# A fused four-block attention kernel: the gates of groups 0 and 1 share one switch of ScalarE's tables inside the FFN, q of group 1 and k's transposes move into the middle of round 0, and the last FFN rows move back

## The chip, the cores and the metric

The kernel runs on one core of a Trainium2 chip. The metric is the device time of one execution in microseconds (us); lower is better. TensorE is PE, VectorE is DVE, ScalarE is ACT, GpSimd is POOL.

## The reference

The input `x` is 32 sequences of 64 tokens with 128 features (2,048 tokens). It passes four blocks:

```python
x = L0(x, ctx)   # layer norm, cross attention, 16 heads of 8, quantised weights
x = L1(x, ctx)   # self attention, cross attention, FFN 128 -> 512 -> 128 with gelu; a layer norm after each
x = L2(x, ctx)   # a gate, three iterations of which only the last counts:
                 #   fused = text + sigmoid(Wg_t @ text_proj + Wg_v @ (r * vision) + bg) * (r * vision)
                 #   with r = softmax over the 64 tokens of 2 * agreement; then a layer norm
x = L3(x, ctx)   # rms norm, rope attention (16 heads of 64, 4 kv heads), rms norm, silu MLP 128 -> 512 -> 128
```

## The kernel before

The tokens are cut into eight groups (`NG`) of 256 tokens (`TG` = 2 tiles of 128). Every engine has a list of steps that is written out by hand and runs in that order; engines meet at semaphores alone, and a step that waits holds all that stands behind it on its engine.

1. L0 and the two attentions of L1 take 24 passes, up to about 220 us of the trace. The change does not touch them.
2. The FFN of L1 follows, group by group. PE runs `mlp_in(g)` (two transposes), `mlp_up(g)` (L531) and `mlp_down(g)` (L544); ACT copies (`f_in`, L858) and takes `gelu(g)` (L867); DVE adds, takes statistics (`ffn_sum`, L1325 and L1275 to L1280) and writes the normed rows (`ffn_rows`, L1334 and L1339) once POOL has the root (L1660). `FT` = 4 tiles of 128 make the 512.
3. Between them PE fills banks with work of the next blocks for the first groups (the tables `EARLY_A`, `EARLY_B`). `RAMP` brings in group 0's q.
4. Then come rounds. Round r has two halves; each does one tile of 128 tokens of L3's attention for group r. It also does L2 for group r + 2, q for group r + 1 and the MLP of group r - 1. `OPENING` lists the two halves of round 0, `HALVES` those of all later rounds, which are alike.

The names in these tables, each with its PE work, its reader and what stands between:

- `l_in`, `l_text`, `l_gate`, `l_back`: L2. PE transposes x (L610), multiplies (L639), multiplies for agreement and gate (L646, L648). ACT copies the bank (`read`, L981, L983, L987). Then `l2_max` (DVE, L1399), `l2_exp` (ACT, L921), `l2_gate` (DVE, L1409), `l2_logits` (POOL, L1813 and L1816), `l2_tanh` (ACT, L930), `l2_weigh` (DVE, L1418), `l2_fuse` (POOL, L1823 and L1827); `l_back` transposes the result `fus` back, and `l2_stats`, `l2_rstd`, `l2_rows` norm it (DVE, POOL, DVE). Group g needs all of these, one after another.
- `k`, `v` (L625), then rope on k: `rotate_k` (DVE, L1477 and L1480), `sum_k` (POOL, L1802 and L1805), and the transposes `kt`, `ks` on PE (L610), copied by ACT (L995).
- `in`: rms norm of L3: `sq3` (ACT, L941), `rms_mean` (DVE, L1449), `rms_power` (POOL), `rms` (ACT, L959), two transposes, a copy (L975). `q0` to `q3` (PE, L617) need it, and DVE reads each with rope (L1463).
- `s0`, `s1`: scores of one tile (PE, L713 to L733) into two banks. `smax3` (DVE, L1519 and L1521), `exps3` (ACT, L1014), `sum3` (DVE), `probs3` (POOL, L1786), `t0`, `t1` (PE transposes, L742), `evac_t3` (ACT, L1020), `pv0`, `pv1` (PE, L756), `evac_pv3` (ACT, L1027), `out` (PE, L633), read by DVE (L1485).

PSUM has eight banks. From `RAMP` on, the uses take them in a ring (`RING3`), so each use waits until the use eight places ahead of it has been read; the early uses take two banks in turn:

```python
def ring_bank(n):
    return (4, 7)[n % 2] if n < NEARLY else RING3[(n - NEARLY) % len(RING3)]
```

Gelu and exp lie in different tables of ACT. The program holds an ACT_TABLE_LOAD where the set changes. Tanh runs after either without a load of its own, as the lists below show.

Of the kernel before, what the change touches and what calls it, by code (L numbers as in the profile page):

```python
# [28 lines left out]
NG = B // GB  # L29
# [57 lines left out]
def build(nc, dr, out):  # L87
    with ExitStack() as ctx:
# [106 lines left out]
        sq = sb("sq", [128, 2, D])  # L195
        ss3 = sb("ss3", [128, 2, TG])
# [36 lines left out]
        def row(name, n=TG):  # L233
# [558 lines left out]
        def _(act):  # L792
# [237 lines left out]
            def opening():  # L1030
                exps3(0)
                l2_tanh(1)
                read("v", 1)
                exps3(1)
                read("k", 2)
                read("l_in", 2)
                read("v", 2)
                exps3(2)
                read("l_back", 1)
                exps3(3)  # L1040
                evac_t3(0)
                read("l_text", 2)
                evac_t3(1)
                read("l_gate", 2)
                sq3(1)
                l2_exp(2)
                evac_pv3(0)
                evac_pv3(1)
                rms(1)
                read("in", 1)  # L1050
                l2_tanh(2)
                evac_t3(2)
# [4 lines left out]
            def first_half(r):  # L1057
# [4 lines left out]
                if 1 <= r < NG - 1:  # L1062
                    sq3(r + 1)
# [68 lines left out]
            l2_exp(0)  # L1132
            f_in(5)
            read("l_in", 1)
            gelu(4)
            l2_tanh(0)
            read("kt", 0)
            f_in(6)
            read("ks", 0)
            gelu(5)  # L1140
            read("l_text", 1)
            read("k", 1)
            gelu(6)
# [17 lines left out]
        def _(dve):  # L1161
# [395 lines left out]

            def first_half(r):
# [400 lines left out]
```

## Time and profile before

| what | us |
|---|---|
| median of 3 runs (502.46 to 503.14) | 502.51 |
| the profiled execution, its own time | 503.35 |
| its span, first to last instruction | 501.4 |
| busy in the span: PE, DVE | 451.1, 377.4 |
| busy in the span: ACT, POOL | 298.6, 273.3 |

1.95 us of the profiled execution's time lie outside its span, and the profiled execution is 0.84 us above the median. "Busy" for PE counts modelled ends of pipelined matmuls, so PE's start times are the better measure: the distance from one start to the next is what a step costs PE. Each fp32 matmul of the program appears twice in the trace (two passes), so a step of four matmuls shows as x8. A row's bracket is the idle time of the engine ahead of it and who ended it.

### The profile page before, as it was taken

Reading aid. Unit: us, or ns where it says so; the run is one execution under the profiler, and the core shown is the slowest. Engines: PE = TensorE matmul, PEld = TensorE weight load, DVE = VectorE, ACT = ScalarE, POOL = GpSimd, SP = SyncE. Lnnn points to the kernel's source line nnn. Section 1 sums busy time; section 2 is a strip of 40 time slices with the busy share of each in tenths; the row PEclk is TensorE's granted clock in tenths of the full one; section 3 lists DMA queues with packets and bytes.
Section 4 is the critical chain, followed back from the end, with each engine's and each line's share of the span. In section 5 each row is a group of like instructions: output and inputs, shape, how many; then the busy total and the mean of one; then the engine's idle time right before and its main releaser. Section 6 shows DMA issues by size and latency. Waiting matters only on the chain.

```text
span 501.4 us, 16946 instructions
## 1 busy us (share of the span) xinstructions
PE 451.1 (90%) x6872; PEld 358.1 (71%) x6872; DVE 377.4 (75%) x918; ACT 298.6 (60%) x724; POOL 273.3 (54%) x332
## 2 busy tenths in 40 slices
PE   4798899999998999899968598999999999999885
PEld 4466666766666776688866377888888888878674
DVE  6699877688988888887687765868777677867642
ACT  2377676767777776757743536565565556553531
POOL 6464877579867787964443534445353545431210
PEclk9799999999999999999989698999999999999999
DMA  8970000000000000000000000000000000000000
GB/s 273 237 244 3 2 3 3 2 3 3 1 4 3 2 3 3 1 1 2 2 0 3 2 1 2 3 12 3 12 3 1 13 3 12 1 13 3 14 1 21
DMA packets 12420, 11.54 MB, mean 23 GB/s; under 512 B 5176, under 2 KB 10296, under 8 KB 12344
## 3 DMA queue, kind: packets, MB, share of 16 engines
q1 hardware_dynamic: 11624, 9.01, 6.9%
q10 hardware_dynamic: 720, 1.45, 0.8%
q8 instruction: 55, 0.90, 0.8%
q14 instruction: 21, 0.17, 0.1%
HBM read 9.42 MB, written 1.05 MB: 21 GB/s over the span
## 4 chain that ended last, share of the span: by engine, by line
PE 49%; DVE 25%; issue 14%; POOL 6%; ACT 4%; DMA 1%; DVEq 0%; POOLq 0%; ACTq 0%
DVE negm L1244 8%; PE ps L617 5%; PE ps L633 5%; DVE blocks L1235 5%; PE ps L733 5%; PE ps L447 4%; PE ps L655 4%; PE ps L465 3%; PE ps L625 2%; PE ps L610 2%; PE ps L495 2%; PE ps L663 2%; PE ps L756 2%; PE ps L407 2%; PE ps L408 2%
## 5 line engine op out<-in xcount | busy, mean ns | idle before, releaser
L1244 DVE TENSOR_REDUCE negm<-ps 128x8 bf16<-128x512 f32 x96 | 59.6, 683 | 25.2 <-PE ps L447 25.1
L832 ACT ACTIVATE p<-ps 128x512 f32<-128x512 f32 x96 | 54.5, 595 | 28.2 <-PE ps L455 27.1
L838 ACT ACTIVATE shared<-ps 128x512 f32<-128x512 f32 x96 | 57.0, 601 | 21.7 <-PE ps L465 20.3
L1733 POOL TENSOR_TENSOR wide<-wide,cv 128x1024 f32<-128x1024 f32 x24 | 45.6, 1901 | 32.6 <-ACT wide L822 32.6
L465 PE MATMUL ps<-cst,p 128*128 128x128 f32 x384 | 58.5, 276 | 0.4 <-ACT shared L838 0.4
L1660 POOL TENSOR_TENSOR rstd<-veps,neghalf 128x2 f32<-128x2 f32 x40 | 29.5, 738 | 49.2 <-DVE veps L1280 30.7
L1786 POOL TENSOR_TENSOR probs<-p,rc 128x512 f32<-128x512 f32 x32 | 33.0, 1044 | 40.6 <-DVE rc L1530 40.5
L465 PEld LDWEIGHTS ps<-cst,p 128*128 128x128 f32 x384 | 44.2, 141 | 11.5 <-issue 9.4
L1027 ACT ACTIVATE late<-ps 128x512 f32<-128x512 f32 x32 | 17.3, 592 | 31.5 <-PE ps L756 31.5
L633 PEld LDWEIGHTS ps<-wo,late 128*128 128x128 f32 x256 | 33.5, 206 | 3.5 <-issue 2.8
L633 PE MATMUL ps<-wo,late 128*128 128x128 f32 x256 | 33.9, 290 | 2.2 <-ACT late L1027 2.2
L617 PE MATMUL ps<-shared,wq 128*128 128x256 f32 x128 | 30.6, 383 | 3.5 <-ACT shared L975 3.4
L1519 DVE TENSOR_REDUCE mx<-ps 128x8 f32<-128x512 f32 x32 | 21.9, 686 | 15.5 <-PE ps L733 15.5
L455 PE MATMUL ps<-negm,idb 128*128 128x512 bf16 x96 | 29.2, 383 | 4.7 <-DVE negm L1244 4.7
L655 PE MATMUL ps<-in_t,wg 128*128 128x256 f32 x128 | 30.0, 380 | 0.7 <-ACT in_t L977 0.7
L617 PEld LDWEIGHTS ps<-shared,wq 128*128 128x128 f32 x128 | 23.1, 190 | 7.5 <-issue 3.3
L1235 DVE TENSOR_TENSOR blocks<-ps,rv 64x128 f32<-64x128 f32 x96 | 27.4, 286 | 1.0
L479 PEld LDWEIGHTS ps<-shared,blocks 128*32 128x32 f32 x1536 | 22.5, 110 | 7.6 <-ACT shared L838 6.4
L447 PE MATMUL ps<-wide,blocks 32*64 32x256 f32 x768 | 27.7, 397 | 0.0
L479 PE MATMUL ps<-shared,blocks 128*32 128x64 f32 x1536 | 26.4, 221 | 0.9 <-ACT shared L838 0.5
L655 PEld LDWEIGHTS ps<-in_t,wg 128*128 128x128 f32 x128 | 23.6, 190 | 3.7 <-issue 0.9
L1014 ACT ACTIVATE p<-p 128x512 f32<-128x512 f32 x32 | 20.2, 635 | 9.4 <-DVE p L1521 9.0
(202 smaller groups left out, 1153.0 us busy)
## 6 DMA issues: line engine op xcount, KB each, us to landing
late<-in_mask_l SPq DMA_DIRECT2D x2, 512.0 KB, 11.8
result<-x_all SPq DMA_DIRECT2D x8, 128.0 KB, 1.8
x_all<-in_x_tok SPq DMA_DIRECT2D x1, 768.0 KB, 7.6
wide<-in_ctx_t SPq DMA_DIRECT2D x1, 768.0 KB, 9.0
rv<-in_rv ACTq DMA_DIRECT2D x1, 768.0 KB, 7.9
wa<-in_wa SPq DMA_DIRECT2D x1, 512.0 KB, 9.5
w<-in_w SPq DMA_DIRECT2D x2, 256.0 KB, 7.7
wq<-in_wq SPq DMA_DIRECT2D x1, 512.0 KB, 7.6
```

Of the source, the lines that this page charges most:

```text
L447: ins = mm(ps[b2 * S:b2 * S + S, S_BANK[r], t * 256:t * 256 + 256], q_t[rows[r], w % 2, cols], r_op[rows[r], w % 2, :, cols], start=(ph == ...
L465: ins = nc.tensor.transpose(bank[:, c * 128:c * 128 + 128], p3[:, n % 3, c * 128:c * 128 + 128], ident)
L479: ins = mm(N[32 * c:32 * c + 32, (t * 2 + b2) * 128:(t * 2 + b2) * 128 + 128] .rearrange("p (h y q) -> p h y q", h=2, y=2)[:, :, x, :], v_ ...
L617: ins = mm(bank_of(f"q{i}", g)[:, j * GT:j * GT + GT], wq3[:, 2 * i + j, :], hn_t[:, g % 2, :], start=True, stop=True, skip_group_check=True)
L633: ins = mm(bank_of("out", n)[:, 0:128], a3_t[:, g % 2, i, u * 128:u * 128 + 128], wo3[:, i, :], start=(i == 0), stop=(i == 7), skip_group_ ...
L655: ins = mm(bank_of(("mg", "mu")[j] + str(i), g)[:, c * GT:c * GT + GT], wg3[:, j, f * 128:f * 128 + 128], hm_t[:, g % 2, :], start=True, s ...
L832: A_(p3[:, n % 3, :], ps[:, S_BANK[r], :], ACT.Exp, scale=SC8).then_inc(sm["act_exp"], 1)
L838: A_(pt[:, w % 2, r, :], pt_bank(RG * w + r), ACT.Copy).then_inc(sm["act_pt"], 1)
L1235: ins = V.tensor_tensor(dst.rearrange("p (t m) d -> p t m d", t=TG), src, bias.unsqueeze(1).to_broadcast([S, TG, NP, DH]), ALU.add)
L1244: V.tensor_reduce(negm[:, n % 4, :], ps[:, S_BANK[r], :].rearrange("p (a k) -> p a k", k=S), AX.X, ALU.max, negate=True).then_inc(sm["dve_ ...
L1733: P.tensor_tensor(r_op[:, w % 2, :, :], k_t[:, w % 2, :].unsqueeze(1).to_broadcast([128, 4, GT]), head_masks.unsqueeze(2).to_broadcast([12 ...
L1786: P.tensor_tensor(probs[:, t % 2, :].rearrange("p (a k) -> p a k", k=S), p3[:, t % 3, :].rearrange("p (a k) -> p a k", k=S), rc3[:, t % 3, ...
```

## The change

It adds and removes no matmul, and adds one exp of a single column (`first_exp`). It moves steps:

- In the FFN, `l_in`, `l_text` and `l_gate` of group 1 come two to three groups earlier. `l2_exp(0)` and `l2_exp(1)` now both run between `gelu(4)` and `gelu(5)`. `v` and `l_back` of group 1, and `in` of group 0, also come inside the FFN; `kt` and `ks` of group 1 leave it.
- In round 0, `kt`, `ks`, `in`, `q0`, `q1` of group 1 stand in the first half, among scores and transposes. A dummy exp ahead of the round brings the table switch to a place of its own.
- `ffn_rows` of groups 6 and 7 leave the FFN loop: they stand late in DVE's list of round 0. `ffn_sum` of group 7 comes after the reading of q of group 0.
- In round 1, `sq3(2)` and `rms_mean(2)` stand a little later.

The hunks below are, in this order: the tables of PE's order; ScalarE's opening; VectorE's opening; VectorE's FFN loop; GpSimd's opening; GpSimd's steps inside the FFN.

```diff
-        EARLY_A = {2: (("k", 0),), 3: (("v", 0), ("l_text", 0)), 5: (("kt", 0), ("ks", 0)),
-                   6: (("l_gate", 1), ("l_back", 0))}
-        EARLY_B = {2: (("l_in", 0),), 3: (("l_gate", 0),), 4: (("l_in", 1),), 5: (("l_text", 1), ("k", 1)),
-                   7: (("kt", 1), ("ks", 1))}
+        EARLY_A = {2: (("k", 0),), 3: (("v", 0), ("l_text", 0)), 4: (("l_text", 1),), 5: (("kt", 0), ("ks", 0)),
+                   6: (("k", 1), ("l_back", 0)), 7: (("l_back", 1),)}
+        EARLY_B = {2: (("l_in", 0),), 3: (("l_gate", 0), ("l_in", 1)), 4: (("l_gate", 1),), 6: (("v", 1),), 7: (("in", 0),)}
...
         OPENING = (
-            (("s0", 0), ("s1", 0), ("s0", 1), ("s1", 1), ("v", 1), ("k", 2), ("l_in", 2), ("v", 2), ("l_back", 1),
-             ("t0", 0), ("l_text", 2), ("t1", 0), ("l_gate", 2)),
...
+            (("s0", 0), ("s1", 0), ("kt", 1), ("ks", 1), ("k", 2), ("l_in", 2), ("s0", 1), ("s1", 1), ("v", 2), ("in", 1),
+             ("t0", 0), ("q0", 1), ("q1", 1), ("t1", 0), ("l_text", 2)),
...
-        RAMP = (("in", 0), ("q0", 0), ("q1", 0), ("q2", 0), ("q3", 0))
+        RAMP = (("q0", 0), ("q1", 0), ("q2", 0), ("q3", 0))
@@ -1028,28 +1028,28 @@
+                A_(first_exp[:, :], neghalf[:, 0:1], ACT.Exp)
+                read("kt", 1)
+                read("ks", 1)
+                sq3(1)
                 exps3(0)
-                l2_tanh(1)
-                read("v", 1)
...
@@ -1530,30 +1533,27 @@
-                l2_gate(1)
                 smax3(0)
                 smax3(1)
-                l2_weigh(1)
+                rms_mean(1)
                 sum3(0)
                 sum3(1)
                 smax3(2)
-                rotate_k(2)
                 smax3(3)
-                l2_stats(1)
+                read("q0", 1)
+                read("q1", 1)
+                l2_max(2)
                 sum3(2)
                 sum3(3)
...
+                rotate_k(2)
                 l2_gate(2)
+                read("q2", 1)
+                read("q3", 1)
+                ffn_rows(NG - 2)
                 read("out", 0)
                 l2_weigh(2)
...
+                ffn_rows(NG - 1)
                 l2_stats(2)
@@ -1617,35 +1619,40 @@
             for i in range(4):
                 read(f"q{i}", 0)
+            ffn_sum(NG - 1)
+            l2_rows(1)
             opening()
@@ -1842,14 +1849,11 @@
-                l2_logits(1)
-                l2_fuse(1)
+                rms_power(1)
                 probs3(0)
                 probs3(1)
-                l2_rstd(1)
                 probs3(2)
                 probs3(3)
-                rms_power(1)
                 sum_k(2)
@@ -1882,10 +1886,14 @@
                 if g == 5:
                     l2_fuse(0)
+                    l2_logits(1)
+                    l2_rstd(0)
+                    l2_fuse(1)
                 if g == 6:
-                    l2_rstd(0)
+                    rms_power(0)
+                if g == 7:
+                    l2_rstd(1)
                     sum_k(1)
-                    rms_power(0)
```

ScalarE inside the FFN, from the first table load to the second gelu behind it, before. L921 is `l2_exp`, L867 `gelu`, L930 `l2_tanh`, L858 `f_in`:

```order
L921 ACT_TABLE_LOAD
L921 ACTIVATE ex,exs<-o_t,agm 128x64 x4
L858 ACTIVATE in_t<-ps 128x256
L981 ACTIVATE a_t<-ps 128x256
L867 ACT_TABLE_LOAD
L867 ACTIVATE shared<-ps,cv 128x256 x4
L930 ACTIVATE gate<-gp,bgh 128x256
L995 ACTIVATE wide<-ps 128x512
L858 ACTIVATE in_t<-ps 128x256
L995 ACTIVATE wide<-ps 128x512
L867 ACTIVATE shared<-ps,cv 128x256 x4
```

The same engine and place in the changed kernel:

```order
L867 ACTIVATE shared<-ps,cv 128x256 x4
L983 ACTIVATE tp_t<-ps,cv 128x256
L858 ACTIVATE in_t<-ps 128x256
L921 ACT_TABLE_LOAD
L921 ACTIVATE ex,exs<-o_t,agm 128x64 x4
L987 ACTIVATE o_t<-ps 128x512
L995 ACTIVATE wide<-ps 128x512 x2
L858 ACTIVATE in_t<-ps 128x256
L921 ACTIVATE ex,exs<-o_t,agm 128x64 x4
L930 ACTIVATE gate<-gp,bgh 128x256
L867 ACT_TABLE_LOAD
L867 ACTIVATE shared<-ps,cv 128x256 x4
```

The first gelu of the lower list is `gelu(4)` and now stands ahead of the load; both exps and a tanh stand between the loads, ahead of `gelu(5)`.

TensorE from the second-last `mlp_down` to the first scores, before. L544 is `mlp_down`, L610 with `kc` and `kcs` is `kt`, `ks` of group 1, L610 with `shared` is `in` of group 0, L617 its q:

```order
L544 MATMUL ps<-w,shared 128x128 x8
L610 MATMUL ps<-cst,kc 128x128 x4
L610 MATMUL ps<-cst,kcs 128x128 x4
L544 MATMUL ps<-w,shared 128x128 x8
L610 MATMUL ps<-cst,shared 128x128 x2
L617 MATMUL ps<-shared,wq 128x256 x8
```

The same place in the changed kernel:

```order
L610 MATMUL ps<-cst,fus 128x128 x2
L544 MATMUL ps<-w,shared 128x128 x8
L610 MATMUL ps<-cst,shared 128x128 x2
L544 MATMUL ps<-w,shared 128x128 x8
L617 MATMUL ps<-shared,wq 128x256 x8
```

`kt` and `ks` are gone from here, `in` of group 0 stands ahead of the last `mlp_down`, and `l_back` of group 1 (`fus`) ahead of the second last.

TensorE at the end of round 0, before, from the values (L756) to the scores of round 1 (L713):

```order
L756 MATMUL ps<-probs_t,blocks 64x256 x8
L610 MATMUL ps<-cst,shared 128x128 x2
L633 MATMUL ps<-wo,late 128x128 x8
L617 MATMUL ps<-shared,wq 128x256 x4
L742 MATMUL ps<-cst,probs 128x128 x8
L610 MATMUL ps<-cst,fus 128x128 x2
L617 MATMUL ps<-shared,wq 128x256 x4
L610 MATMUL ps<-cst,kc 128x128 x4
L610 MATMUL ps<-cst,kcs 128x128 x4
L713 MATMUL ps<-m3a,idb 128x512 x2
```

In the changed kernel:

```order
L756 MATMUL ps<-probs_t,blocks 64x256 x8
L617 MATMUL ps<-shared,wq 128x256 x4
L742 MATMUL ps<-cst,probs 128x128 x4
L633 MATMUL ps<-wo,late 128x128 x8
L742 MATMUL ps<-cst,probs 128x128 x4
L610 MATMUL ps<-cst,fus 128x128 x2
L610 MATMUL ps<-cst,kc 128x128 x4
L610 MATMUL ps<-cst,kcs 128x128 x4
L713 MATMUL ps<-m3a,idb 128x512 x2
```

Half of q of group 1 (one L617 row of 4) and `in` (L610 with `shared`) left this stretch, and nothing but `kt`, `ks` stands between `l_back` (L610 with `fus`) and the scores.

## Rows read from the trace of the kernel before

**Rows 1.** Windows: stretch, length, busy PE, PEld, DVE, ACT, POOL, clock, DMA, GB/s.
```profile
231.00:261.00 30.00, 25.43 (x164) 22.44 (x163) 22.36 (x73) 18.24 (x49) 16.29 (x21) 0.94 0.00 1
261.00:293.30 32.30, 25.37 (x367) 19.97 (x368) 24.32 (x57) 14.99 (x45) 14.28 (x18) 0.84 0.01 2
293.30:310.00 16.70, 14.33 (x212) 12.13 (x209) 9.87 (x23) 8.90 (x26) 5.61 (x7) 0.90 0.01 2
310.00:450.00 140.00, 136.36 (x2134) 115.54 (x2134) 106.94 (x226) 84.36 (x234) 64.97 (x80) 1.00 0.03 7
```

**Rows 2.** The timeline of PE, last FFN groups: start, length, instruction, idle before.
```profile
231.80 1.89 PE L531 MATMUL ps<-in_t,w 128*128 128x256 f32 x8
233.53 0.38 PE L520 MATMUL ps<-cst,x_all 128*128 128x128 f32 x2
233.74 1.95 PE L544 MATMUL ps<-w,shared 128*128 128x128 f32 x16
235.53 0.38 PE L610 MATMUL ps<-cst,x_all 128*128 128x128 f32 x2
...
255.31 0.63 PE L610 MATMUL ps<-cst,kc 128*128 128x128 f32 x4 [3.05 <-POOL kc L1805]
...
256.96 3.15 PE L544 MATMUL ps<-w,shared 128*128 128x128 f32 x16 [0.28 <-DVE y L1325]
...
260.99 3.69 PE L617 MATMUL ps<-shared,wq 128*128 128x256 f32 x16 [0.66 <-ACT shared L975]
```

**Rows 3.** The timeline of ScalarE (ACT), the same stretch and the first exp of round 0.
```profile
232.67 1.28 ACT L921 ACT_TABLE_LOAD   x1
...
236.44 1.28 ACT L867 ACT_TABLE_LOAD   x1
237.74 1.57 ACT L867 ACTIVATE shared<-ps,cv 128x256 f32<-128x256 f32 x4
240.53 0.51 ACT L930 ACTIVATE gate<-gp,bgh 128x256 f32<-128x256 f32 x1 [1.22 <-POOL gp L1816]
...
269.67 0.63 ACT L1014 ACTIVATE p<-p 128x512 f32<-128x512 f32 x1 [6.08 <-DVE p L1521]
```

**Rows 4.** The timeline of GpSimd (POOL): the first gate, then k and gate of round 0.
```profile
244.37 0.73 POOL L1827 TENSOR_TENSOR fus<-fus,a_t 128x256 f32<-128x256 f32 x1
...
252.33 1.49 POOL L1802 TENSOR_TENSOR kcs<-kc,wa 128x256 f32<-128x256 f32 x2 [0.20 <-DVE wa L1480]
...
285.08 1.45 POOL L1802 TENSOR_TENSOR kcs<-kc,wa 128x256 f32<-128x256 f32 x2
286.61 1.26 POOL L1805 TENSOR_TENSOR kc<-kc,wa 128x512 f32<-128x512 f32 x1
...
292.25 0.73 POOL L1827 TENSOR_TENSOR fus<-fus,a_t 128x256 f32<-128x256 f32 x1
```

**Rows 5.** The timeline of VectorE (DVE): stalled rows, q, the first row maximum.
```profile
253.28 2.03 DVE L1339 SCALAR_TENSOR_TENSOR x_all<-yg,rstd,rv 128x128 f32<-128x128 f32 x2
...
262.33 2.35 DVE L1463 TENSOR_TENSOR wide<-ps,cst 128x1024 f32<-128x1024 f32 x2
...
268.22 0.69 DVE L1519 TENSOR_REDUCE mx<-ps 128x8 f32<-128x512 f32 x1 [0.93 <-PE ps L733]
```

**Rows 6.** The timeline of PE, round 0 and the start of round 1.
```profile
279.99 1.94 PE L646 MATMUL ps<-tp_t,vp 128*128 128x64 f32 x8 [0.95 <-ACT tp_t L983]
...
287.33 0.66 PE L610 MATMUL ps<-cst,shared 128*128 128x128 f32 x2 [2.53 <-ACT shared L959]
...
293.26 0.38 PE L610 MATMUL ps<-cst,fus 128*128 128x128 f32 x2
...
296.08 0.59 PE L713 MATMUL ps<-m3a,idb 128*128 128x512 bf16 x2
...
302.51 0.67 PE L639 MATMUL ps<-a_t,wl 128*128 128x256 f32 x2 [2.25 <-ACT a_t L981]
```

**Rows 7.** The page, costliest groups: a probability tile on POOL.
```profile
L1786 POOL TENSOR_TENSOR probs<-p,rc 128x512 f32<-128x512 f32 x32 | 33.0, 1044 | 40.6 <-DVE rc L1530 40.5
```

More of the change, by code:

```diff
@@ L195, in build @@
         sq = sb("sq", [128, 2, D])
+        first_exp = sb("first_exp", [128, 1])
         ss3 = sb("ss3", [128, 2, TG])
@@ L1030, in opening @@
             def opening():
+                A_(first_exp[:, :], neghalf[:, 0:1], ACT.Exp)
+                read("kt", 1)
+                read("ks", 1)
+                sq3(1)
                 exps3(0)
-                l2_tanh(1)
-                read("v", 1)
-                exps3(1)
                 read("k", 2)
                 read("l_in", 2)
+                exps3(1)
+                rms(1)
                 read("v", 2)
+                read("in", 1)
+                evac_t3(0)
                 exps3(2)
-                read("l_back", 1)
                 exps3(3)
-                evac_t3(0)
+                evac_t3(1)
                 read("l_text", 2)
-                evac_t3(1)
                 read("l_gate", 2)
-                sq3(1)
+                evac_pv3(0)
                 l2_exp(2)
-                evac_pv3(0)
                 evac_pv3(1)
-                rms(1)
-                read("in", 1)
+                evac_t3(2)
                 l2_tanh(2)
-                evac_t3(2)
                 read("l_back", 2)
@@ L1068, in first_half @@
                     exps3(2 * n)
+                if r == 1:
+                    sq3(2)
                 if r + 2 < NG:
@@ L1131, in _ @@
             read("l_gate", 0)
-            l2_exp(0)
-            f_in(5)
             read("l_in", 1)
             gelu(4)
+            read("l_text", 1)
+            f_in(5)
+            l2_exp(0)
+            read("l_gate", 1)
+            read("kt", 0)
+            read("ks", 0)
+            f_in(6)
+            l2_exp(1)
             l2_tanh(0)
-            read("kt", 0)
-            f_in(6)
-            read("ks", 0)
             gelu(5)
-            read("l_text", 1)
             read("k", 1)
+            read("l_back", 0)
+            f_in(7)
+            l2_tanh(1)
             gelu(6)
-            read("l_gate", 1)
-            f_in(7)
-            read("l_back", 0)
+            read("v", 1)
+            read("l_back", 1)
+            sq3(0)
             gelu(7)
-            sq3(0)
-            read("kt", 1)
-            read("ks", 1)
             rms(0)
             read("in", 0)
-            l2_exp(1)
             opening()
@@ L1571, in first_half @@
                     smax3(2 * n + 1)
+                if r == 1:
+                    rms_mean(2)
                 if r == NG:
@@ L1619, in ahead_of_sum @@
                     rotate_k(0)
+                if g == 5:
+                    l2_stats(0)
+                    l2_weigh(1)
                 if g == 6:
-                    l2_rows(0)
-                if g == 7:
-                    l2_max(1)
+                    rms_mean(0)
             def ahead_of_rows(g):
@@ L1629, in ahead_of_rows @@
                     l2_gate(0)
+                    l2_max(1)
                 if g == 4:
                     l2_weigh(0)
+                    l2_gate(1)
                 if g == 5:
-                    l2_stats(0)
+                    l2_rows(0)
+                if g == 6:
+                    l2_stats(1)
                     rotate_k(1)
-                if g == 6:
-                    rms_mean(0)
-            for g in range(NG):
+            for g in range(NG - 1):
                 ahead_of_sum(g)
```

14 lines of the change are left out of this document (3 added, 11 removed), and 4 rows, old and new, of the table OPENING.

## Prediction

> **What bounds the kernel now.** I read three views, in this order. First the windows [rows 1]: from 310 to 450 us, in the even rounds, PE is busy for 136.36 of 140 us at full clock. There the kernel is bound by PE, the order of work is unchanged, and whatever is won ahead of round 1 is kept. In the two stretches from 231 to 293.3 us, the last FFN groups and round 0, PE is busy for 25.4 of 30 and 25.4 of 32.3 us, at a granted clock of 0.94 and 0.84. No other engine is full there either; DVE comes next with 22.4 and 24.3 us. So this part is bound by waits along a chain of engines, and by the lower clock that follows PE's idle times.
>
> Second, PE's timeline of the FFN [rows 2]. From start to start an `mlp_up` costs 1.73 us and an `mlp_down` 1.79 us at full clock. PE loses time late: 3.05 us ahead of `kt` of group 1, which waits for POOL's `sum_k`, and then the last `mlp_down` takes 3.15 us instead of 1.95, which is the clock at its lower level (1.2 against 2.4 GHz). q of group 0 starts at 260.99.
>
> Third, PE's timeline of round 0 [rows 6], up to the start of round 1. The agreement matmuls at 279.99 take 1.94 us, about twice their full-clock cost; 2.53 us go ahead of `in` of group 1; `l_back` of group 2 is at 293.26, the scores of round 1 start at 296.08.
>
> **Part 1, to q of group 0.** PE's own work from 231.80 to the start of q, at full clock, is four `mlp_up` (6.9), five `mlp_down` (9.0) and 5.7 of small pieces, 21.6 us. Before, 29.2 us pass (260.99 - 231.80), so 7.6 are waits and clock. The change takes `kt` and `ks` out (0.9) and puts `v` and `l_back` of group 1 in (1.1): 21.8 us of work, earliest start 253.6. Now the waits.
>
> The chain to the first gate: ACT takes `l_gate` of group 0 at 232.0, then `l_in` of group 1, `gelu(4)` (1.57, at 237.74 in [rows 3]), `l_text`, `f_in(5)`, and reaches the table load at about 235.4 instead of 232.67. The load is 1.28 us and the gelu at 237.74 starts right after its own [rows 3]. `l2_exp(0)` takes 1.4 (to 238.1). Then `l_gate` of group 1, `kt`, `ks` and `f_in(6)` must be copied; PE delivers `ks` at 240.3, so `l2_exp(1)` starts near 241.3, ends at 242.7, and the tanh (0.5) ends at 243.1, where it ended at 241.04 before [rows 3]. The second load and `gelu(5)` end at 246.05, 0.5 ahead of the `mlp_down` that needs it. From tanh to `fus` took 4.06 us before (241.04 to 245.10, [rows 3, 4]); here DVE's `ffn_sum(4)` stands ahead of `l2_weigh` for 0.6, but the idle time in that path is shorter, so 2.9 us: `fus` at 246.05. PE is free for `l_back` at 244.7: it waits 1.3.
>
> The second gate follows on POOL without a gap (`fus` at 250.35) and PE comes for it at 251.0: no wait. Then `l2_rows(0)`, `sq3`, `ffn_rows(5)`, `rms_mean`, `rms_power` (0.7) and `rms` (0.7) stand ahead of `in` of group 0: DVE is through at 253.2, `hn` is ready at 255.1, and PE, free at 253.0, waits 2.1. Sum: 253.6 + 1.3 + 2.1 = 257.0; with 0.2 for meetings of engines 257.2. That is 3.8 earlier. A wait of 2.1 us may lower the clock, as 2.25 us did near 302 (the stretch 293.3 to 310 has 0.90, [rows 1, 6]). I take it that it does: the last `mlp_down` then costs 1.2 more, as at 256.96 [rows 2], and q starts at 258.4.
>
> Behind q stands DVE: four rope reads, 2.35 for two [rows 5], about 4.5 in all. Then `ffn_sum(7)` (1.3) and `l2_rows(1)` (1.2), both new at this place, and only then the first row maximum: 257.2 + 1.0 + 4.55 + 2.5 = 265.3, or 266.5 with the low clock; before it was 268.22 [rows 5]. Of 3.8 us DVE's new steps take back 0.9. **Term 1: -2.9 at full clock, -1.7 at low clock; I take -1.7.**
>
> `ffn_rows(6)` leaves the path here. Two of its instructions took 2.03 us before, while POOL's `kcs` ran beside them from 252.33 [rows 4, 5]; they are 0.61 alone. The Trainium skill says why ("SBUF — State Buffer", section on the shared port pair: whichever of a two-input DVE operation and a GpSimd operation starts first holds the pair and the other blocks fully), and the trace agrees with it here. By this row a meeting of such steps costs up to 1.4 us: I charge 1.0 more for the new meetings as the end of the range, nothing in the sum.
>
> **Part 2, from the first row maximum (T) to `l_back` of group 2.** Before: 293.26 - 268.22 = 25.0 us. After, with the durations of this trace: four `smax3` and two sums on DVE, with exps between, end at T + 7.2. The new `in`, `q0`, `q1` of group 1 are done on PE by T + 7.4, under them. `exps3`, a copy and `l_text` on ACT: T + 8.9. `l_gate` on PE at T + 9.0, 1.35: at T + 10.35. Here PE has no idle time over 0.7, so I take full clock, where before it took twice as long at 279.99 [rows 6]. Copy 0.6, maximum 0.55, and behind it `sum3` twice, then POOL's `probs3` twice (1.04 each, [rows 7]): T + 14.7. `sum_k` is 2.8 (285.08 to 287.87, [rows 4]): T + 17.5, at most T + 18 when it meets `rotate_k`. `l2_logits` 1.4, tanh 0.5, `l2_weigh` 0.4 behind `ffn_rows(6)`, which may meet POOL (0.4), `l2_fuse` 1.4, steps between engines 0.2: T + 22.3. **Term 2: -2.7.** PE idles for about 6 us at the end of it, from T + 16.4: the values are long done, and nothing else is in its list.
>
> **Part 3, to round 1.** Between `l_back` and the scores stood `q2`, `q3`, `kt`, `ks`, 2.82 us (293.26 to 296.08, [rows 6]); now `kt` and `ks`, 1.1. **Term 3: -1.7.** But PE comes out of 6 us of idle time. Before, the work that followed the gap of 3.05 was slow at 256.96 and at full speed again at 260.99 [rows 2]: some 4 us at half speed once PE works again. That costs `kt`, `ks` and the scores some 2.0 us. **Term 4: +2.0.** In round 1 `sq3(2)` now stands ahead of `l_in` of group 3, which had PE wait for 2.25 at 302.51 [rows 6]: **term 5: +0.2.** The rest of the rounds is as before.
>
> Moved at no cost: the dummy exp and its load (1.5 us) lie in ACT's wait for the scores, which was 6.08 us ahead of 269.67 [rows 3]; without it the load would delay the first exp by 1.3.
>
> Sum: -1.7 - 2.7 - 1.7 + 2.0 + 0.2 = -3.9, and -5.1 if PE's clock holds ahead of q. I take the value between, -4.5: the profiled execution would go from 503.35 to 498.85. It stands 0.84 above the median of the runs, so the median goes from 502.51 to 498.0.
>
> One rule speaks for less. The Trainium skill ("ScalarE: Activation LUTs", what a table load costs) puts a drain of 1.38 us beside the load of 1.28. With it the two loads inside the FFN would make `gelu(5)` 2.8 later, 2.3 past its slack of 0.5, and the sum -2.2. In the trace the gelu at 237.74 starts 0.02 after its load ends [rows 3]: no drain shows behind the load, and I go by the row.
>
> **The rivals.**
> A, the forecast: gain of 3 to 6.5 us, chance 0.55.
> B, a larger gain: the clock holds ahead of q (-5.1 in all) and the idle time ahead of `l_back` lowers it for less than 2 us: -5.1 - 2.0 = -7.1, with fewer meetings of DVE and POOL than I counted (0.5) -7.6. For it: the gap of 0.28 and 0.66 ahead of 260.99 did not lower it. Chance 0.18.
> C, a small gain: the clock stays low through the scores and values of round 1, as it did for most of 280 to 290 (+2 more), or each gate's links are slower: -1 to -3. Chance 0.13, in it 0.03 for the drain.
> D, no effect: the waits only move, and the 6 us of idle time ahead of `l_back` become 10. Chance 0.05.
> E, slower: the gate chain inside the FFN is late. Five links of it now stand in order ahead of `ffn` steps on ACT, DVE and POOL (`l2_rstd(0)` ahead of `f_res(7)`), and each late link holds PE and the FFN too. If each gate takes from the load to `fus` the 12.4 us of group 0 before (232.67 to 245.10, [rows 3, 4]) instead of my 10.65, and the second likewise, q starts 3.5 later; it decides the sign from 4.5 on. With twice that, +7.0: 505.0. Against it: POOL is busy for only 16.3 of 30 us there [rows 1]. Chance 0.09.
>
> **The numbers.** This kernel's runs tell 0.2% (1.0 us) from no change. Faster: A, B, C = 0.86; same 0.05; slower 0.09. Range: at the low end B, -7.6 and 0.6 for rounding of many small links, 494.3; at the high end C's -1.5, 501.0. It leaves out D, E and half of C.
>
> **What would show it.** Right: three table loads, the first near 235.4; q of group 0 at 257 to 258.5; first row maximum at 265 to 266.5; PE idle 5 to 6 us ahead of `l_back` of group 2, which starts near 288; scores of round 1 near 290 and at half speed. Wrong: PE waiting over 2.5 us at `l_back` of group 0 or 1, `gelu(5)` past 246.6, or a clock below 0.9 in windows after round 1 that were at 1.00.

## The result, and the profile after

The changed kernel takes 498.87 us (median of 5 runs, 498.52 to 500.32) against 502.51 for the kernel before, run beside it (5 runs, 501.44 to 503.49). The ratio is 0.9935, with an interval of 0.9918 to 0.9951: faster by 3.6 us, where 4.5 was forecast. The profiled execution takes 500.22, its span 498.3, so 3.13 less than the 503.35 of before. The two traces are equal up to the FFN (the first L479 of PE starts at 28.34 and at 28.32), and times can be compared as they stand.

TensorE's timeline after, for the FFN's end, the end of round 0 and the start of round 1 (start, length, instruction, idle time before and its releaser):

```profile
246.25 0.41 PE L610 MATMUL ps<-cst,fus 128*128 128x128 f32 x2 [1.24 <-POOL fus L1834]
...
251.09 0.39 PE L610 MATMUL ps<-cst,fus 128*128 128x128 f32 x2
...
255.41 0.66 PE L610 MATMUL ps<-cst,shared 128*128 128x128 f32 x2 [2.14 <-ACT shared L959]
255.86 3.35 PE L544 MATMUL ps<-w,shared 128*128 128x128 f32 x16
...
290.91 0.66 PE L610 MATMUL ps<-cst,fus 128*128 128x128 f32 x2 [6.28 <-POOL fus L1834]
...
293.07 1.06 PE L713 MATMUL ps<-m3a,idb 128*128 128x512 bf16 x2
...
297.29 1.04 PE L756 MATMUL ps<-probs_t,blocks 64*64 64x256 f32 x16
...
301.00 0.67 PE L639 MATMUL ps<-a_t,wl 128*128 128x256 f32 x2 [2.30 <-ACT a_t L981]
...
302.37 1.95 PE L633 MATMUL ps<-wo,late 128*128 128x128 f32 x16
304.16 1.00 PE L646 MATMUL ps<-tp_t,vp 128*128 128x64 f32 x8
```

They answer to [rows 2] and [rows 6]. PE waits 1.24 us for the gate of group 0 (`fus`), not at all for that of group 1 (251.09), and 2.14 for `in` of group 0. The last `mlp_down` (255.86) takes 3.35 us, as 3.15 in [rows 2]. The wait ahead of `l_back` of group 2 has grown from nothing to 6.28 us, and the first operations behind it take about twice the time they had before: the first two scores 1.06 us instead of 0.59 [rows 6]. The clock is at the lower level, 1.2 GHz, there: the window from 290.9 to 295.0 us has a granted clock of 0.50.

ScalarE's timeline after, beside [rows 3]:

```profile
235.59 1.28 ACT L921 ACT_TABLE_LOAD   x1
...
243.10 1.28 ACT L867 ACT_TABLE_LOAD   x1
244.39 1.57 ACT L867 ACTIVATE shared<-ps,cv 128x256 f32<-128x256 f32 x4
...
256.60 1.28 ACT L1031 ACT_TABLE_LOAD   x1
257.89 0.20 ACT L1031 ACTIVATE first_exp<-neghalf 128x1 f32<-128x1 f32 x1
```

There are three table loads, each followed at once (within 0.01 us) by its function. Nothing shows a drain, in three more cases of what [rows 3] showed.

VectorE's timeline after, beside [rows 5]:

```profile
252.42 0.61 DVE L1337 SCALAR_TENSOR_TENSOR yg<-y,mv,rv 128x128 f32<-128x128 f32 x2 [0.34 <-POOL rstd L1667]
253.07 0.61 DVE L1342 SCALAR_TENSOR_TENSOR x_all<-yg,rstd,rv 128x128 f32<-128x128 f32 x2
...
253.67 0.42 DVE L1328 TENSOR_TENSOR y<-ps,resb 128x256 f32<-128x256 f32 x1
...
256.38 0.75 DVE L1483 TENSOR_TENSOR wa<-kk,cst 128x256 f32<-128x256 f32 x2
...
267.09 0.68 DVE L1522 TENSOR_REDUCE mx<-ps 128x8 f32<-128x512 f32 x1
```

The same place before, four rows that the prediction did not have. L1477 and L1480 are the rotation of k of group 1 (`rotate_k(1)`), 250.89 to 252.17:

```profile
250.89 0.69 DVE L1477 TENSOR_TENSOR kc<-kk,cst 128x512 f32<-128x512 f32 x1
...
252.17 1.07 DVE L1334 SCALAR_TENSOR_TENSOR yg<-y,mv,rv 128x128 f32<-128x128 f32 x2
...
256.40 0.42 DVE L1325 TENSOR_TENSOR y<-ps,resb 128x256 f32<-128x256 f32 x1
...
259.32 0.61 DVE L1334 SCALAR_TENSOR_TENSOR yg<-y,mv,rv 128x128 f32<-128x128 f32 x2 [1.49 <-POOL rstd L1660]
```

L1339 at 253.28 with its 2.03 us [rows 5] follows L1334 at 252.17. In both kernels the row instructions (L1334 and L1339, now L1337 and L1342) are `ffn_rows(5)`; those of 259.32 are `ffn_rows(6)`. Before, `ffn_rows(5)` takes 3.1 us, and `ffn_sum(6)`, for which the last `mlp_down` waits, starts at 256.40. After, it takes 1.2 us, `ffn_sum(6)` starts at 253.67, and the rotation of k (L1483) stands behind it. So DVE's line ahead of `ffn_sum(6)` has lost two things: 1.3 us of the rotation itself, and 1.9 us by which the rows were longer beside POOL's sum of k.

Windows after, from q of group 0 to `l_back` of group 2, from there into round 1, and 140 us of the rounds (columns as in [rows 1]):

```profile
259.00:290.90 31.90, 23.54 (x378) 18.64 (x378) 27.81 (x53) 12.41 (x34) 12.28 (x14) 0.98 0.01 2
290.90:308.00 17.10, 14.25 (x205) 11.66 (x206) 8.25 (x25) 9.85 (x31) 5.61 (x7) 0.84 0.00 1
308.00:448.00 140.00, 136.77 (x2207) 115.97 (x2208) 106.69 (x223) 83.22 (x229) 65.08 (x80) 1.00 0.03 7
```

The clock is 0.98 in round 0 (0.84 before), and lower in the stretch that begins with `l_back` of group 2 (0.84, before 0.90). In the 140 us behind it PE is busy for 136.77 us at full clock, as for 136.36 before.

### The profile page after: what moved, and what is told of

Its sections match the earlier page's. It is cut to its first block, busy times and chain, and to the rows that moved or that the text cites. A ratio compares the mean times of both kernels' runs of the same rounds, so it can differ in the third digit from the quotient of the medians.

```text
span 498.3 us, 16947 instructions
## 1 busy us (share of the span) xinstructions
PE 447.4 (90%) x6872; PEld 355.5 (71%) x6872; DVE 378.3 (76%) x918; ACT 299.4 (60%) x725; POOL 274.5 (55%) x332
## 4 chain that ended last, share of the span: by engine, by line
PE 54%; DVE 22%; issue 13%; POOL 6%; ACT 4%; DMA 1%; DVEq 0%; POOLq 0%; ACTq 0%
DVE negm L1247 8%; PE ps L733 5%; PE ps L617 5%; DVE blocks L1238 5%; PE ps L447 4%; PE ps L633 4%; PE ps L655 4%; PE ps L465 3%; PE ps L610 3%; PE ps L625 2%; PE ps L544 2%; PE ps L531 2%; PE ps L495 2%; PE ps L756 2%; PE ps L663 2%
## 5 line engine op out<-in xcount | busy, mean ns | idle before, releaser
L1740 POOL TENSOR_TENSOR wide<-wide,cv 128x1024 f32<-128x1024 f32 x24 | 45.6, 1902 | 32.5 <-ACT wide L822 32.5
L1027 ACT ACTIVATE late<-ps 128x512 f32<-128x512 f32 x32 | 17.5, 594 | 35.9 <-PE ps L756 35.9
L617 PE MATMUL ps<-shared,wq 128*128 128x256 f32 x128 | 30.7, 384 | 3.5 <-ACT shared L975 3.4
L633 PE MATMUL ps<-wo,late 128*128 128x128 f32 x256 | 31.3, 275 | 2.2 <-ACT late L1027 2.2
L633 PEld LDWEIGHTS ps<-wo,late 128*128 128x128 f32 x256 | 30.7, 192 | 3.4 <-issue 2.8
L617 PEld LDWEIGHTS ps<-shared,wq 128*128 128x128 f32 x128 | 23.1, 190 | 7.9 <-issue 3.7
L479 PEld LDWEIGHTS ps<-shared,blocks 128*32 128x32 f32 x1536 | 22.5, 110 | 7.6 <-ACT shared L838 6.5
L479 PE MATMUL ps<-shared,blocks 128*32 128x64 f32 x1536 | 26.4, 220 | 0.9 <-ACT shared L838 0.5
L1020 ACT ACTIVATE probs_t<-ps 128x512 f32<-128x512 f32 x32 | 18.9, 595 | 8.2 <-PE ps L742 7.9
```

The source lines that it names most:

```text
L479: ins = mm(N[32 * c:32 * c + 32, (t * 2 + b2) * 128:(t * 2 + b2) * 128 + 128] .rearrange("p (h y q) -> p h y q", h=2, y=2)[:, :, x, :], v_ ...
L617: ins = mm(bank_of(f"q{i}", g)[:, j * GT:j * GT + GT], wq3[:, 2 * i + j, :], hn_t[:, g % 2, :], start=True, stop=True, skip_group_check=True)
L633: ins = mm(bank_of("out", n)[:, 0:128], a3_t[:, g % 2, i, u * 128:u * 128 + 128], wo3[:, i, :], start=(i == 0), stop=(i == 7), skip_group_ ...
L1740: P.tensor_tensor(r_op[:, w % 2, :, :], k_t[:, w % 2, :].unsqueeze(1).to_broadcast([128, 4, GT]), head_masks.unsqueeze(2).to_broadcast([12 ...
```

## The experiments

All times are medians, with range and number of runs. Ratios are to the kernel before, run on the same chip beside each set of four experiments (its medians were 502.77, 502.31 and 502.85). Where a trace's opening is earlier, as in three of these profiles (last section), I compare by distances to an anchor in the trace.

**The idle time ahead of `l_back` filled.** Is the slow stretch of 291 to 297 us paid for by PE's idle time? The matmuls added write to a bank that the next operation overwrites; the computation is unchanged.

```diff
+            BUSY = {("l_back", 2): 26}
...
+                for _ in range(BUSY.get((what, g), 0)):
+                    mm(bank_of(what, g)[:, 0:128], ones[:, :], ones[:, :], start=True, stop=True, skip_group_check=True)
```

> The changed kernel with 26 extra 128x128 matmuls on PE (their result is overwritten) in its idle time of 6.28 us ahead of l_back of group 2. Theory, the clock: the kt, ks, scores that follow this idle time ran at the lower clock and lost 2.5 us (2.16 instead of 1.09 and 4.22 instead of 2.76); PE kept busy there, they run at full clock and the kernel gets 2.0 to 2.5 us faster than the changed one, about 496.6. Rival: what follows waits for other engines anyway, so the 2.5 us come back as a longer wait ahead of l_text of group 3 (2.3 us now): 498.9, no change.

Measured: 496.08 (495.83 to 500.14, 6 runs), ratio 0.9887 [0.9857, 0.9917]. Its TensorE timeline:

```profile
284.47 5.97 PE L691 MATMUL ps<-ones 128*128 128x128 f32 x52
290.84 0.44 PE L610 MATMUL ps<-cst,fus 128*128 128x128 f32 x2 [0.40 <-POOL fus L1838]
...
291.99 0.59 PE L717 MATMUL ps<-m3a,idb 128*128 128x512 bf16 x2
...
294.75 1.05 PE L760 MATMUL ps<-probs_t,blocks 64*64 64x256 f32 x16
```

`l_back` starts where it did, and from scores to values pass 2.76 us instead of 4.22: in the trace 2.5 us are won by round 1. The wait ahead of `l_text` of group 3 is 2.29 us, as it was (2.30), so the rival is out: the low clock behind the gap is a cost of its own.

**The FFN part alone**, round 0 in the old order.

```diff
         OPENING = (
-            (("s0", 0), ("s1", 0), ("kt", 1), ("ks", 1), ("k", 2), ("l_in", 2), ("s0", 1), ("s1", 1), ("v", 2), ("in", 1),
...
+            (("s0", 0), ("s1", 0), ("s0", 1), ("s1", 1), ("kt", 1), ("ks", 1), ("k", 2), ("l_in", 2), ("v", 2),
...
+            (("pv0", -1), ("pv1", -1), ("in", 1), ("out", -1), ("q0", 1), ("q1", 1), ("t0", 0), ("t1", 0),
+             ("l_back", 2), ("q2", 1), ("q3", 1), ("kt", 2), ("ks", 2)),
```

The lists of the other engines for round 0 follow it.

> The FFN part of the change alone, with round 0 ordered as before (kt and ks of group 1 behind the second scores; in, q0, q1 of group 1 in the second half). Theory: the FFN part gives what the first row maximum shows, 1.1 to 1.3 us; the other two thirds of the gain lie in round 0. So 501.2, within 0.3% of the kernel before. Rival: the FFN part carries the whole gain, since v and l_back of group 1 are out of round 0 and its first half is shorter: 499, as the changed kernel.

Measured: 498.79 (497.38 to 499.93, 6 runs), ratio 0.9922 [0.9902, 0.9943]. No part of the gain is gone.

```profile
294.30 0.59 PE L713 MATMUL ps<-m3a,idb 128*128 128x512 bf16 x2
...
297.06 1.05 PE L756 MATMUL ps<-probs_t,blocks 64*64 64x256 f32 x16
```

The scores come at 294.30, 1.23 later than in the changed kernel, and the values at 297.06, 0.23 earlier: without a gap ahead of `l_back` they run at full clock. The new order of round 0 wins 1.2 us up to the scores and gives them back at the low clock.

**The end of round 0 in another order.** `l2_logits` goes ahead of `sum_k` on POOL and `l2_gate` ahead of `rotate_k` on DVE, so that the gate no longer stands behind k; `l2_weigh` goes ahead of the last FFN rows, and `kt`, `ks` ahead of `l_back` on PE. What each of these moves is worth alone was not tried.

```diff
-             ("l_back", 2), ("kt", 2), ("ks", 2)),
+             ("kt", 2), ("ks", 2), ("l_back", 2)),
...
-                rotate_k(2)
                 l2_gate(2)
+                rotate_k(2)
...
-                sum_k(2)
                 l2_logits(2)
+                sum_k(2)
                 l2_fuse(2)
```

> The changed kernel with the tail of round 0 in another order: GpSimd does l2_logits of group 2 ahead of sum_k instead of behind it, VectorE l2_gate ahead of rotate_k and l2_weigh ahead of the FFN rows, PE kt and ks ahead of l_back. Theory: l_back of group 2 waits for POOL's line probs3, sum_k, logits, fuse and ScalarE's tanh between; with the logits first, the tanh lies under sum_k and the scores of round 1 start about 4 us earlier: 495 (494.3 to 496.5). Rival: DVE's reads of q2 and q3 (until 286.8) then hold the weighing and little is won: -1, 498.

Measured: 495.3 (494.11 to 497.07, 4 runs), ratio 0.986 [0.9836, 0.9885]. The profiled execution had an earlier opening, by 1.72 us at `l_back` of group 0.

```profile
253.69 0.41 PE L610 MATMUL ps<-cst,shared 128*128 128x128 f32 x2 [2.13 <-ACT shared L959]
253.94 1.95 PE L544 MATMUL ps<-w,shared 128*128 128x128 f32 x16
255.72 3.62 PE L617 MATMUL ps<-shared,wq 128*128 128x256 f32 x16
...
284.58 1.09 PE L610 MATMUL ps<-cst,kc 128*128 128x128 f32 x4 [3.28 <-POOL kc L1812]
...
286.86 1.06 PE L713 MATMUL ps<-m3a,idb 128*128 128x512 bf16 x2
```

The gap is 3.28 us, now ahead of `kt`, instead of 6.28 ahead of `l_back`, and the scores stand at 286.86 + 1.72 = 288.58, 4.5 earlier. Of that 2.9 lie behind q (31.14 us from q to the scores, for 34.02 with the change), and 1.6 ahead of it, most of it the `mlp_down` at 253.94, which ran at full clock here though the gap ahead of it is as long.

**The same with the three gaps filled**, with the loop of the first experiment:

```diff
+            BUSY = {("in", 0): 9, ("kt", 2): 14, ("l_text", 3): 9}
```

> The kernel with the reordered tail (495.3 in its first runs, 494.1 to 497.1) and extra matmuls in the three gaps of PE: 9 ahead of in of group 0, 14 ahead of kt of group 2, 9 ahead of l_text of group 3. Theory: the kt, ks, l_back, scores behind the second gap go at full clock (they took 6.62 us from 284.58 to 291.20, 4.1 at full clock), and the other two gaps lose their lower clock in the executions that have it: 492 to 493. Rival: the extra matmuls end too late or the work behind waits for others anyway: 495.

Measured: 494.99 (494.44 to 496.06, 5 runs), ratio 0.9862 [0.9841, 0.9882]. The median did not move, the rival's value. By its trace the values of round 1 stand 45.4 us behind `l_back` of group 0, where they stood 46.7 behind it without the matmuls: 1.3 us won, less than forecast. `l_back` of group 2, which waited for nothing there, now waits 0.82 us for the gate.

**Only the gap ahead of `in` of group 0 filled** in the changed kernel, with the same loop:

```diff
+            BUSY = {("in", 0): 9}
```

> The changed kernel with 9 extra matmuls on PE in its idle time of 2.14 us ahead of in of group 0. In the profile of the changed kernel the last mlp_down behind this gap took 3.35 us (lower clock), in that of the tail kernel, behind the same gap, 1.95. Theory: this gap lowers the clock in some executions and not in others, and that makes the two levels of the runs (500.2 and 498.5). Filled, the last mlp_down always takes 1.95, and all runs lie at the lower level: median 498.4, runs within 0.5 us. Rival: the levels come from another place, for example from the gap ahead of l_text of group 3; then the spread of 1.8 us stays and the median is 498.9.

Measured: 499.03 (497.54 to 501.63, 7 runs), ratio 0.9938 [0.9916, 0.9961]. In the trace the last `mlp_down` takes 1.95 and q starts at 257.11, but the runs still spread, over 4.1 us (1.8 in the five runs of the change), and their median is that of the change. So this gap's clock does not make the spread.

**Is it the last rows?** The kernel before with `ffn_rows(6)` moved into round 0 alone:

```diff
-                if g < NG - 1:
+                if g < NG - 2:
                     ffn_rows(g)
```

> The kernel before with one part of the change: ffn_rows of group 6 out of the FFN, next to those of group 7 late in round 0. Theory: these four instructions took 3.1 us beside GpSimd's kcs and kc and stood ahead of l2_rows of group 0, sq3, rms and in of group 0, but PE was held by kt behind GpSimd's kc until 255.16 all the same; so q starts at most 0.7 us earlier, and in round 0 the four cost 1.2 in front of l_back: 502.0 to 502.8, no change. Rival: DVE's line is what PE waits for; q starts 2 us earlier, 500.5.

Measured: 502.24 (500.78 to 503.35, 12 runs), ratio 0.9989 [0.9975, 1.0002]. No change. And the changed kernel with these rows back in the FFN:

```diff
-                ffn_rows(NG - 2)
                 read("out", 0)
...
-                if g < NG - 2:
+                if g < NG - 1:
                     ffn_rows(g)
```

> The changed kernel with the FFN rows of group 6 back in the FFN, where DVE waits 2.98 us for q. Theory: they stand still beside GpSimd's sum_k until about 260, just as q comes (+0.2), and what they leave free in round 0 is not waited for, since the tanh is ready only at 288.45 and l2_weigh starts at 288.81 (-0.3): no change, 498.9. Rival: the rows late in round 0 are what makes l_back of group 2 late (1.8 us): 497.2.

Measured: 500.22 (498.14 to 502.04, 7 runs), ratio 0.995 [0.9931, 0.9969], which overlaps the change's. Its trace has 31.81 us from q to `l_back`, against 31.86. These rows are worth nothing that can be measured.

**Is it `kt` and `ks`?** The kernel before with both taken out of the FFN and put behind the second scores of round 0:

```diff
-        EARLY_B = {2: (("l_in", 0),), 3: (("l_gate", 0),), 4: (("l_in", 1),), 5: (("l_text", 1), ("k", 1)),
-                   7: (("kt", 1), ("ks", 1))}
+        EARLY_B = {2: (("l_in", 0),), 3: (("l_gate", 0),), 4: (("l_in", 1),), 5: (("l_text", 1), ("k", 1))}
```

> The kernel before with kt and ks of group 1 moved out of the FFN, behind the second scores of round 0, and nothing else. PE waited 3.05 us for them. Theory: the wait is handed on: the last mlp_down needs ffn_sum of group 6, which DVE has at 256.8 only (it stands behind the FFN rows of group 6 and l2_rows of group 0), so q of group 0 starts at most 0.5 us earlier: 502.3, no change. Rival: the wait for kt is the cost, q starts 2 us or more earlier: 500.5.

Measured: 501.75 (500.42 to 503.31, 12 runs), ratio 0.9991 [0.9976, 1.0006]. No change. With the edit of `ffn_rows(6)` on top of it (the first under the last rows):

> The same with ffn_rows of group 6 late as well: two small edits of the change, no gate moved. Theory: the two waits stood side by side ahead of q (kt behind GpSimd's k sum, ffn_sum of group 6 behind the rows); each alone wins nothing, both together let q start near 257.4 to 258.5 as in the changed kernel, so 499.5 to 500.5, which is most of the gain without the shared table switch. Rival: the gates inside the FFN are what wins; without them q starts no earlier than 260: 502.

Measured: 502.59 (501.47 to 504.04, 12 runs), ratio 1.0009 [0.9995, 1.0022]. I expected most of the gain, and got none. Its PE, then its DVE:

```profile
256.95 3.76 PE L543 MATMUL ps<-w,shared 128*128 128x128 f32 x16 [4.71 <-DVE y L1324]
```

```profile
253.27 2.03 DVE L1338 SCALAR_TENSOR_TENSOR x_all<-yg,rstd,rv 128x128 f32<-128x128 f32 x2
```

PE's wait of 3.05 for `kc` has become one of 4.71 for `y`. The rows with their 2.03 us are still there, though `ffn_rows(6)` has left: that showed me that they belong to group 5. `ffn_sum(6)` still starts at 256.39, so what delays it stands in this stretch of DVE's line: k's rotation, and whatever makes the rows slow.

**k of group 1 late, and no gate moved.** The kernel of the last experiment (`kt`, `ks` and `ffn_rows(6)` late) with one more edit: `rotate_k(1)` behind `ffn_sum(6)` and `sum_k(1)` behind the rms of group 0:

```diff
                     l2_stats(0)
-                    rotate_k(1)
                 if g == 6:
                     rms_mean(0)
+                    rotate_k(1)
...
                     l2_rstd(0)
-                    sum_k(1)
                     rms_power(0)
+                if g == 7:
+                    sum_k(1)
```

> The kernel before with k of group 1 late and no gate moved: kt and ks of group 1 behind the second scores of round 0, its rotate_k on DVE and sum_k on GpSimd behind ffn_sum of group 6, and the FFN rows of group 6 late. Theory: what held the last mlp_down until 256.8 was not an FFN row of its own cost but rotate_k (1.3 us) and the rows of group 5 that stand still beside GpSimd's sum_k (3.1 us where 1.2 are needed), all ahead of ffn_sum of group 6. With k behind it, ffn_sum of group 6 comes near 253.7 as in the changed kernel, q starts at 257.5 to 258.5, and the kernel is 2 to 3 us faster than before: 499.5 to 500.5, most of the gain. Rival: the gates in the FFN are what gives the time: 502.

Measured: 497.32 (497.22 to 498.17, 4 runs), ratio 0.9898 [0.9882, 0.9914]. Its trace, whose opening is earlier (by 1.53 us at the `mlp_down` of group 3, 232.21 against 233.74 before):

```profile
249.43 0.61 DVE L1333 SCALAR_TENSOR_TENSOR yg<-y,mv,rv 128x128 f32<-128x128 f32 x2
250.08 0.61 DVE L1338 SCALAR_TENSOR_TENSOR x_all<-yg,rstd,rv 128x128 f32<-128x128 f32 x2
...
251.78 0.42 DVE L1324 TENSOR_TENSOR y<-ps,resb 128x256 f32<-128x256 f32 x1
```

```profile
252.35 2.02 PE L543 MATMUL ps<-w,shared 128*128 128x128 f32 x16 [1.63 <-DVE y L1324]
...
256.30 3.69 PE L616 MATMUL ps<-shared,wq 128*128 128x256 f32 x16 [0.66 <-ACT shared L974]
...
294.53 1.05 PE L755 MATMUL ps<-probs_t,blocks 64*64 64x256 f32 x16
```

The rows of group 5 take 0.61 each and the last `mlp_down` waits 1.63 us. With 1.53 added, q starts at 257.83 and the values at 296.06, against 259.05 and 297.29 with the change. The whole gain is there, without a gate moved. That the median is even lower than the change's (498.87) is in part the opening, if the runs are like the profiled one.

**The opposite: the change with k of group 1 early again.**

```diff
                 if g == 5:
+                    rotate_k(1)
                     l2_rows(0)
                 if g == 6:
                     l2_stats(1)
-                    rotate_k(1)
...
                 if g == 6:
+                    sum_k(1)
                     rms_power(0)
                 if g == 7:
                     l2_rstd(1)
-                    sum_k(1)
```

> The changed kernel with rotate_k of group 1 back ahead of l2_rows of group 0, and sum_k of group 1 ahead of rms_power of group 0 on GpSimd, as before; the gates and all of PE's order stay. Theory: q of group 0 starts 2 to 3 us later than in the changed kernel, and that is the gain of the FFN part: 501 to 502. Rival: the gates' part carries the gain and k's place is free: 499.

Measured: 503.44 (501.51 to 504.92, 12 runs), ratio 1.0012 [1.0, 1.0024]. The whole gain is gone. Its DVE, POOL and PE:

```profile
249.98 0.69 DVE L1480 TENSOR_TENSOR kc<-kk,cst 128x512 f32<-128x512 f32 x1
250.59 1.82 DVE L1483 TENSOR_TENSOR wa<-kk,cst 128x256 f32<-128x256 f32 x2
...
252.96 1.58 DVE L1447 SCALAR_TENSOR_TENSOR x_all<-wide,rstd,rv 128x128 f32<-128x128 f32 x2
254.47 1.68 DVE L1337 SCALAR_TENSOR_TENSOR yg<-y,mv,rv 128x128 f32<-128x128 f32 x2
...
256.78 0.42 DVE L1328 TENSOR_TENSOR y<-ps,resb 128x256 f32<-128x256 f32 x1
```

```profile
252.95 1.45 POOL L1809 TENSOR_TENSOR kcs<-kc,wa 128x256 f32<-128x256 f32 x2
254.47 1.26 POOL L1812 TENSOR_TENSOR kc<-kc,wa 128x512 f32<-128x512 f32 x1
```

```profile
258.53 0.66 PE L610 MATMUL ps<-cst,shared 128*128 128x128 f32 x2 [4.94 <-ACT shared L959]
...
262.40 1.93 PE L617 MATMUL ps<-shared,wq 128*128 128x256 f32 x7
```

L1447 and L1337 on DVE take 1.58 and 1.68 for their two instructions while `kcs` and `kc` run on POOL from 252.95 to 255.73; in the changed kernel's trace L1447 has 0.96 and L1337 0.61. `ffn_sum(6)` starts at 256.78, 3.1 us later than with the change, and q 3.35 us later. The larger part of the 3.1 is the rotation itself: it holds DVE from 249.98 to 252.33, 2.35 us (1.3 before), and the rows of group 5 are 1.1 us longer. Whether `rotate_k` or `sum_k` alone, moved back, would cost as much was not tried.

**Without the dummy exp** ahead of the scores:

```diff
             def opening():
-                A_(first_exp[:, :], neghalf[:, 0:1], ACT.Exp)
```

> The changed kernel without the dummy exp: the table load then stands directly ahead of the first exp of round 0, behind the squares. Theory: the load issues as soon as ScalarE has the squares behind it (268.24 in the changed kernel) and ends 1.0 later than the exp could start (268.54), so the first sums come 0.4 to 1.0 later: +0.5, 499.4. Rival: no load waits for anything there and all is hidden: 498.9.

Measured: 498.24 (497.45 to 500.43, 6 runs), ratio 0.9922 [0.9897, 0.9946]. In its trace the load stands at 266.33, ahead of the first exp. That exp comes 1.0 us later behind the start of q (10.50 us for 9.49), where the prediction said 1.3; at `l_back` 0.26 us of it are left (32.12 us for 31.86). The runs show no loss.

## Why the prediction came out right, point by point

The time lies in the range and on the side with 0.86. In the traces, from -4.5 to the measured -3.13:

- **Part 1, the waits.** Forecast 1.3, 0 and 2.1 us, measured 1.24, 0 and 2.14; the first load at 235.59 (235.4), `gelu(5)` through at 245.96 (246.05), the last `mlp_down` at the low clock. q starts at 259.05 (258.4): 0.3 of it ahead of `in`, 0.3 in and around the `mlp_down`. **Term 1** is -1.13 instead of -1.7. To take the value between the sums for the two clock levels was a hedge; in this execution the clock was at the low one.
- **Part 1, the reason.** Here I misread the trace. "`ffn_rows(6)` leaves the path here. Two of its instructions took 2.03 us before": these were `ffn_rows(5)`, which the change leaves where they are. What frees them and `ffn_sum(6)` is that k of group 1, `rotate_k` on DVE and `sum_k` on POOL, moved behind them. The timetable that I drew up had k at its new place, so the sum survived the wrong reason; that part of the forecast came out right without being understood. Adding k late to a version that had gained nothing brought the whole gain, and putting k early again took the whole gain away; moving the rows alone changed nothing. How much of it is the rotation's own time and how much the slow rows, only the traces tell (1.3 and 1.9 us before).
- **The gates** gain nothing by themselves: the version without their move is at least as fast, and with them in place but k early nothing is won. They fit into the FFN as forecast, against rival E.
- **Term 2 was mis-sized**: `l_back` comes at T + 23.82, not T + 22.3, so -1.22 instead of -2.7. The links slipped in two places: ahead of `l_gate`, behind q0 and q1 of group 1 (T + 9.74 for 9.0), and where `rotate_k` and the two probability tiles run side by side and are both longer (1.60 us for L1483, which took 0.75 in the FFN, and 2.49 for two tiles, for which 1.04 each stood). So `sum_k` ends at T + 19.4, for which I wrote 17.5 and summed with 18. The meeting cost that I had kept for the end of the range belonged in the sum.
- **Terms 3 and 4.** -1.73 (forecast -1.7), and +2.53 for the low clock behind the gap (+2.0): `l_back` to scores takes 2.16 us, where 2.82 less 1.73 would be 1.09, and scores to values 4.22 instead of 2.76. Filling the gap gave back 2.5 in the trace and 2.8 between the medians: the mechanism is shown.
- **Term 5** is +0.04 instead of +0.2.
- **Not in the forecast: -1.62.** From `l_text` of group 3 to the agreement matmuls (L646) pass 3.16 us after and 4.78 before, since PE's clock stayed up behind a wait of 2.30 where it had fallen behind 2.25:

```profile
304.04 3.42 PE L633 MATMUL ps<-wo,late 128*128 128x128 f32 x16
307.29 0.89 PE L646 MATMUL ps<-tp_t,vp 128*128 128x64 f32 x7
```

The `out` of 16 rows (L633) takes 3.42 us here and 1.95 after. The measured sum is -1.13 - 1.22 - 1.73 + 2.53 + 0.04 - 1.62 = -3.13. Without this last piece the trace would stand at -1.5, so part of how near the forecast came in the traces is luck. The piece may belong to the one execution of the kernel before: four versions of it (the last rows, `kt`, both, k late) have the same wait of 2.25 or 2.26 us there, and L633 takes 1.95 in each. The medians, 3.6 us apart, are far clear of the noise; which pieces make them up in the executions that were not profiled stays open.
- **The signs.** Of those that I named, the three loads, the first of them near 235.4, and the lower clock behind the last gap came as said. q (259.05), the first row maximum (267.09), `l_back` (290.91) and the scores (293.07) all stand later than their stated places, by 0.6 to 3.1 us, most of it from term 2; the gap of 6.28 us is a little longer than the 5 to 6 that I gave.
- **The rivals.** Of B, C, D and E none happened as told, though C's mechanism (low clock through the scores) did, inside term 4.

Another order of the end of round 0 gives 0.986, the best of all. Joining it to the version with k late and no gate moved was not tried.

## What to carry to other kernels

Before you put a price on moving an instruction, find the group number behind each row: the rows of two groups look alike, and only a count through the order tells them apart. When a wait on the critical path ends at a chain of short two-input operations, look at what runs on GpSimd beside them and at what feeds it, and move that behind the chain. And an idle time on TensorE costs more than itself: order the work so that what the gap waits for comes first, and where a gap of several us is left, try cheap matmuls in it (2.5 us in the trace for a gap of 6.3 here; gaps of 2.1 to 3.3 us, filled in two experiments, moved no median).

## What the runs showed of the hardware that I had not expected

**The same gap lowers the clock in one execution and not in another.** Behind the wait of 2.13 or 2.14 us for `in` of group 0 the last `mlp_down` took 3.35 to 3.49 us in four profiles (the change, the large gap filled, the FFN part alone, the rows back) and 1.95 in two (without the dummy exp, and the reordered end of round 0, shown above at 253.94). Behind 2.25 to 2.43 us at `l_text` L633 took 3.42 us in the profile of the kernel before, 2.97 with the rows back, and 1.95 in the eleven others that have the gap. What decides it stays open.

**The opening varies by 2 us.** The first L479 of PE starts between 28.06 and 28.34 us in eleven profiles and at 26.26 to 26.36 in three. TensorE's timeline of the reordered end, then of the change:

```profile
12.75 0.69 PE L390 MATMUL ps<-cst,wide 128*128 128x128 f32 x2 [0.53 <-DVE wide L1210]
```

```profile
14.53 0.69 PE L390 MATMUL ps<-cst,wide 128*128 128x128 f32 x2 [3.05 <-DVE wide L1210]
```

PE waits 0.53 us for DVE in the one and 3.05 in the other, with the same instructions. The two traces show what makes DVE late. In the change, L1740 on POOL starts at 12.13, L1210 on DVE behind it at 12.30, and L1210 takes 2.17 us. In the reordered end L1210 starts first, at 12.10, takes 0.60 us, and L1740 starts at 12.88. All fourteen profiles fall in line with this (the same two steps, a few lines off in some kernels): in eleven L1740 starts first and a DVE operation behind it takes 1.6 us longer (L1210 in eight, the one ahead of it, 1.89 us instead of 0.29, in three); in the three short openings L1210 is through before L1740 starts. L1740 is late there because two multiplications of PE ahead of it take 1.22 and 1.06 us instead of 0.70 and 0.59: a delay on one engine shortens the opening. No run tried to force either order. A shorter opening would explain much of the spread between the runs of one kernel, but only the profiled executions show theirs, so that is argued.

**GpSimd is stretched too.** Beside DVE's work L1820 on POOL took 0.99 us in the reordered version (279.47) and 0.61 in the change (286.49), and two probability tiles took 2.49 and 2.05 us in one trace (280.59 and 270.80 of the change).
